# A decoder layer on one core: cross attention's projections as 16-bit products, and new places for every step

## Time and profile before

| | us |
|---|---|
| median of three runs | 619.71 |
| the profiled execution | 618.64 |
| its span | 616.8 |
| PE busy | 578.8 (94%) |
| DVE busy | 445.3 (72%) |
| ACT busy | 405.0 (66%) |
| POOL busy | 314.0 (51%) |

### The profile page before, as it was taken

How to read it: one execution, slowest core, us unless ns; L and a number is a source line. 1 busy time by engine, 2 the same in 40 slices (tenths; PEclk the granted TensorE clock), 3 DMA queues, 4 the chain that set the end, 5 groups by cost and what they waited for, 6 DMA issues and landing times. The chain is left out here.

```text
span 616.8 us, 17220 instructions
## 1 busy us (share of the span) xinstructions
PE 578.8 (94%) x6780; PEld 414.5 (67%) x6780; DVE 445.3 (72%) x1504; ACT 405.0 (66%) x520; POOL 314.0 (51%) x199
## 2 busy tenths in 40 slices
PE   6798888999999999999999999999999988899994
PEld 2544644777677877777677767786677756585664
DVE  2467476758897888888887889788878886267456
ACT  1425754796659765886579666976588657866661
POOL 5165432646357444665357544834566536155553
PEclk9898997999999999999999999999999999899999
DMA  6540111010200030002100120003000110000000
GB/s 179 157 138 27 46 49 43 5 30 1 72 14 10 2 91 28 22 2 62 56 21 3 46 73 19 4 2 108 10 22 3 35 55 4 2 19 2 2 18 18
DMA packets 31607, 23.08 MB, mean 37 GB/s; under 512 B 2808, under 2 KB 30216, under 8 KB 31528
## 3 DMA queue, kind: packets, MB, share of 16 engines
q1 hardware_dynamic: 23801, 16.59, 9.2%
q10 hardware_dynamic: 7375, 4.97, 2.7%
q0 software_dynamic: 352, 0.43, 0.4%
HBM read 13.90 MB, written 5.46 MB: 31 GB/s over the span
## 5 line engine op out<-in xcount | busy, mean ns | idle before, releaser
L540 POOL TENSOR_TENSOR gl<-g,gh 128x1024 f16<-128x1024 f32 x96 | 204.1, 2135 | 176.3 <-ACT gh L705 104.3
L716 ACT ACTIVATE g<-ps,b 128x512 f32<-128x512 f32 x256 | 168.5, 686 | 91.8 <-PE ps L1003 90.4
L1372 DVE SCALAR_TENSOR_TENSOR acc<-ps,cw,acc 128x128 f32<-128x128 f32 x448 | 125.9, 344 | 67.6 <-PE ps L1024 50.9
L1022 PE MATMUL ps<-w2h,gh 128*128 128x128 f16 x768 | 133.6, 219 | 1.9 <-DVE acc L1372 1.5
L1024 PE MATMUL ps<-w2h,gl 128*128 128x128 f16 x768 | 133.4, 219 | 0.0
L1023 PE MATMUL ps<-w2l,gh 128*128 128x128 f16 x768 | 133.4, 219 | 0.0
L1001 PE MATMUL ps<-x2h,w1h 128*128 128x512 f16 x256 | 98.6, 385 | 4.8 <-ACT g L716 4.8
L1003 PE MATMUL ps<-x2h,w1l 128*128 128x512 f16 x256 | 98.0, 383 | 0.0
L1002 PE MATMUL ps<-x2l,w1h 128*128 128x512 f16 x256 | 98.0, 383 | 0.0
L1022 PEld LDWEIGHTS ps<-w2h,gh 128*128 128x128 f16 x768 | 75.1, 98 | 18.1 <-issue 10.8
L1023 PEld LDWEIGHTS ps<-w2l,gh 128*128 128x128 f16 x768 | 75.1, 98 | 5.4 <-issue 1.6
(11 more groups left out here) (189 smaller groups left out, 900.2 us busy)
## 6 DMA issues: line engine op xcount, KB each, us to landing
q_rep<-q_parts SPq DMA_DIRECT2D x24, 128.0 KB
x<-in_x SPq DMA_DIRECT2D x8, 256.0 KB, 3.6
w_stage<-in_L_ffn_w ACTq DMA_DIRECT2D x1, 2048.0 KB, 10.9
q_swap<-q SPq DMA_DIRECT2D x16, 128.0 KB, 2.1
q_parts<-qx SPq DMA_DIRECT2D x16, 128.0 KB, 2.1
k_rep<-k_parts SPq DMA_DIRECT2D x24, 77.0 KB
out<-fin SPq DMA_DIRECT2D x7, 256.0 KB, 2.5
g<-in_L_ffn_w ACTq DMA_DIRECT2D x6, 256.0 KB, 3.1
```

Of the source, the lines that this page charges most:

```text
L540: pool.tensor_tensor(gl[:, j % SPLIT_RING, :, :], g32[:, e % RING, :, :], gh[:, j % SPLIT_RING, :, :], ALU.subtract).then_inc(s["lo"], 1)
L716: act.activation(g32[:, e % RING, h, :], bH[:, h, :], ACT.Gelu, bias=b1[:, e, h:h + 1], scale=1.0 / WS).then_inc(s["gelu"], 1)
L1022: pe.matmul(o, ghb, w2h[:, j, h, :], start=(h == 0), stop=False)
L1372: m = dve.scalar_tensor_tensor(out=(acc_all if e == E - 1 else acc)[:, b, :], in0=second_bank(f, e)[:, b * P:(b + 1) * P], scalar=cw[:, b, ...
```

## The change

The four projections no longer run in float32. The weights (`xw`) are split once into `xwh` (ACT, L643's place) and `xwl` (DVE), multiplied by WS = 256; ctx, x1 and the attention output are split as they leave PSUM: the high part by ACT in place of the copy, the low part by DVE in three new steps, `cx_l`, `x1_l` and `ao_l`. Each projection becomes three products into one sum: high by high, low weight by high, high by low. PE waits for the low parts where it waited for the copies. Since the sums carry the factor 256, what reads them divides: v in two DVE instructions instead of one (the operation takes one dimension less), the high parts of k and q in ACT's scale, their low parts in two DVE steps (first k or q in float32 into `k1` or `q1`, then the subtraction), y2 in its own instruction. `q1` lies in `y1`, so the norm waits for `qxl` of the group before. The exps stay whole.

All tables of places are new, and the counts of idle products with them. In the steady bodies the largest moves are: q's projection from place 63 to 55, its x1 transpose from 54 to 49, v from 46 to 53, k from 54 to 59; the query's steps of linear attention to 2 to 6; on PE the second transposed score from 35 to 34 and the third from 39 to 36, on ACT the exps from 32, 38, 39, 40 to 34, 36, 37, 40; ACT's conversion of x (`x_t`) from 3 to 0, ahead of the first gelu (place 1). In the first body ACT's first gelu (`q`) moves from place 15, behind the load places 6 and 8, to place 2, ahead of them; the loads of w2 move to 32, 35, 38 and 64. The diff, cut (of the tables the steady ones whole, of the others what is spoken of):

```diff
-PE_AT = dict(x_t=3, q=7, kv01=8, kv23=22, k_mean=28, kv=32, den=35, out=36, cx_t=43, v1=46, x1_t=54, k=54,
-             q_x=63, scores=(8, 8, 10, 12, 13, 14, 20, 20), max_t=26, scores_t=(29, 35, 39, 40), values=(39, 40,
-             42, 42), wo=55, x2_t=62, logits=0, c_t=57, b2=62, first=3, next=0, second=0, u_t=(43, 45), ao_t=49)
-ACT_AT = dict(x_t=3, q=5, kv23=25, cx_t=42, x1_t=54, k=55, q_x=63, max_t=27, scores_t=(32, 38, 39, 40), x2_t=62,
-              weights=0, c_t=61, gelu=1, high=3, u=(40, 45), ao_t=52)
-DVE_AT = dict(high=3, q=23, kv01=17, kv23=22, k_rot=26, k_mean=26, kv=31, den=33, out=33, norm1=37, norm2=41,
-              x1=49, v1=47, k=57, q_x=63, scores=(5, 8, 9, 11, 15, 16, 20, 20), max=22, pairs=(42, 47), wo=55,
-              x2=59, x2_t=61, logits=0, weights=3, cw=11, b2=61, combine=0, finish=51, q_sin=31, sums=31, xl=1,
-              cw_hl=42)
...
+PE_AT = dict(x_t=2, q=4, kv01=6, kv23=14, k_mean=24, kv=32, den=33, out=35, cx_t=42, v1=53, x1_t=49, k=59,
+             q_x=55, scores=(8, 9, 11, 15, 16, 20, 20, 23), max_t=28, scores_t=(32, 34, 36, 40), values=(36, 38,
+             41, 42), wo=50, x2_t=63, logits=0, c_t=59, b2=63, first=3, next=0, second=0, u_t=(42, 44), ao_t=47)
+ACT_AT = dict(x_t=0, q=2, kv23=24, cx_t=45, x1_t=51, k=58, q_x=55, max_t=30, scores_t=(34, 36, 37, 40), x2_t=63,
+              weights=0, c_t=60, gelu=1, high=3, u=(40, 44), ao_t=46)
+DVE_AT = dict(high=3, q=20, kv01=6, kv23=15, k_rot=25, k_mean=26, kv=29, den=30, out=34, norm1=34, norm2=38,
+              x1=43, v1=53, k=57, q_x=54, scores=(8, 10, 12, 14, 15, 17, 21, 22), max=23, pairs=(43, 43), wo=52,
+              x2=59, x2_t=63, logits=0, weights=2, cw=11, b2=61, combine=0, finish=41, q_sin=26, sums=29, xl=0,
+              cw_hl=30, cx_l=46, x1_l=51, ao_l=48)
...
-ACT_FIRST = dict(x_t=0, q=15, cx_t=24, kv23=22, k=32, x1_t=63, q_x=63)
...
-PE_FILL0 = dict(q=2, kv01=12, kv23=5, k_mean=1, kv=1, den=2, out=0, v1=6, k=0, x1_t=42, q_x=3)
-PE_FILL1 = dict(q=19, kv01=4, kv23=4, scores=0, max_t=0, scores_t=20, kv=2, den=0, out=0, k_mean=7, values=25,
-                wo=2, q_x=1, x2_t=6, v1=3, x1_t=1, u_t=31)
...
+ACT_FIRST = dict(x_t=0, q=2, cx_t=8, kv23=23, k=32, x1_t=59, q_x=63)
...
+PE_FILL0 = dict(q=9, kv01=6, kv23=3, k_mean=3, kv=0, den=0, out=0, v1=11, k=0, x1_t=47, q_x=6)
+PE_FILL1 = dict(q=22, kv01=1, kv23=4, scores=0, max_t=4, scores_t=9, kv=0, den=0, out=1, k_mean=0, values=24,
+                wo=3, q_x=8, x2_t=15, v1=4, x1_t=0, u_t=16)
...
-HIGH_W = (44, 56, 67, 68, 68, 76, 122)
-LOW_W = (76, 78, 80, 80, 92, 96, 124)
-SCALE_W = (119,)
-LOAD_W = (8, 29, 45, 57)
-W1_W = (6,)
-ROWS_W = (17, 59)
...
+HIGH_W = (40, 46, 72, 73, 73, 74, 86)
+LOW_W = (77, 78, 85, 88, 89, 102, 103)
+SCALE_W = (49,)
+LOAD_W = (32, 35, 38, 64)
+W1_W = (2,)
+ROWS_W = (9, 62)
...
                 if p == at["cx_t"]:
+                    if first_group(a):
+                        act.wait_ge(s["ld_xw"], 16 * 4)
+                        act.activation(xwh[:, :, :], xw[:, :, :], ACT.Copy, scale=WS).then_inc(s["i_xw"], 1)
                     since(act, "cx_tp", a + 1)
-                    act.copy(cx_t[:, :], bC[:, 0:B * CTX]).then_inc(s["cx_tc"], 1)
+                    act.copy(cxh[:, :], bC[:, 0:B * CTX]).then_inc(s["cxh"], 1)
                 if p == at["x1_t"]:
                     since(act, "x1_tp", a + 1)
-                    act.copy(x1_t[:, :], bC).then_inc(s["x1_tc"], 1)
+                    act.copy(x1h[:, :], bC).then_inc(s["x1h"], 1)
                 if p == at["k"]:
 
                     since(act, "k_p", a + 1)
                     since(act, "st_k", 16 * a)
-                    act.activation(kx[:, 0, :], bD[:, 0:B * CTX], ACT.Identity, bias=xbk[:, :]).then_inc(s["kxh"], 1)
+                    act.activation(kx[:, 0, :], bD[:, 0:B * CTX], ACT.Identity, bias=xbk[:, :], scale=1.0 / WS).then_inc(s["kxh"], 1)
                 if p == at["q_x"]:
                     since(act, "q_xp", a + 1)
                     since(act, "st_qh", 16 * a)
-                    act.activation(qx[:, 0, :], bC, ACT.Identity, bias=xbq[:, :]).then_inc(s["qxh"], 1)
+                    act.activation(qx[:, 0, :], bC, ACT.Identity, bias=xbq[:, :], scale=1.0 / WS).then_inc(s["qxh"], 1)
 
             def cross(g, p):
                 if p == at["max_t"]:
...
-                    act.copy(ao_t[:, :], bA).then_inc(s["ao_tc"], 1)
+                    act.copy(aoh[:, :], bA).then_inc(s["aoh"], 1)
...
-                    since(pe, "cx_tc", a + 1)
-                    pe.wait_ge(s["ld_xw"], 16 * 4)
-                    for b in range(B):
-                        m = pe.matmul(bD[0:CTX, b * P:(b + 1) * P], cx_t[:, b * CTX:(b + 1) * CTX], xw[:, 2, :], start=True, stop=True)
+                    since(pe, "cxl", a + 1)
+                    pe.wait_ge(s["i_xw"], 2)
+                    for b in range(B):
+                        o, tok = bD[0:CTX, b * P:(b + 1) * P], slice(b * CTX, (b + 1) * CTX)
+                        pe.matmul(o, cxh[:, tok], xwh[:, 2, :], start=True, stop=False)
+                        pe.matmul(o, cxh[:, tok], xwl[:, 2, :], start=False, stop=False)
+                        m = pe.matmul(o, cxl[:, tok], xwh[:, 2, :], start=False, stop=True)
                     m.then_inc(s["v1_p"], 1)
...
-                    pe.matmul(bD[:, 0:B * CTX], xw[:, 1, :], cx_t[:, :], start=True, stop=True).then_inc(s["k_p"], 1)
+                    pe.matmul(bD[:, 0:B * CTX], xwh[:, 1, :], cxh[:, :], start=True, stop=False)
+                    pe.matmul(bD[:, 0:B * CTX], xwl[:, 1, :], cxh[:, :], start=False, stop=False)
+                    pe.matmul(bD[:, 0:B * CTX], xwh[:, 1, :], cxl[:, :], start=False, stop=True).then_inc(s["k_p"], 1)
                 if p == at["q_x"]:
                     fill("q_x")
-                    since(pe, "x1_tc", a + 1)
-                    pe.matmul(bC, xw[:, 0, :], x1_t[:, :], start=True, stop=True).then_inc(s["q_xp"], 1)
+                    since(pe, "x1l", a + 1)
+                    pe.matmul(bC, xwh[:, 0, :], x1h[:, :], start=True, stop=False)
+                    pe.matmul(bC, xwl[:, 0, :], x1h[:, :], start=False, stop=False)
+                    pe.matmul(bC, xwh[:, 0, :], x1l[:, :], start=False, stop=True).then_inc(s["q_xp"], 1)
...
-                    since(pe, "ao_tc", g + 1)
-                    for b in range(B):
-                        m = pe.matmul(bB[:, b * P:(b + 1) * P], ao_t[:, b * P:(b + 1) * P], xw[:, 3, :], start=True, stop=True)
+                    since(pe, "aol", g + 1)
+                    for b in range(B):
+                        o, tok = bB[:, b * P:(b + 1) * P], slice(b * P, (b + 1) * P)
+                        pe.matmul(o, aoh[:, tok], xwh[:, 3, :], start=True, stop=False)
+                        pe.matmul(o, aoh[:, tok], xwl[:, 3, :], start=False, stop=False)
+                        m = pe.matmul(o, aol[:, tok], xwh[:, 3, :], start=False, stop=True)
...
+                    since(dve, "qxl", a)
...
-                    dve.tensor_tensor(of_heads(v_pad[:, :, :]), bD[0:CTX, :].rearrange("p (m j d) -> p m j d", j=2, d=HD),
-                                      bv[0:CTX, :, :].rearrange("p b (m j d) -> p (b m) j d", j=2, d=HD), ALU.add).then_inc(s["v1"], 1)
+                    for j in range(2):
+                        d = dve.scalar_tensor_tensor(out=of_heads(v_pad[:, :, :])[:, :, j, :], in0=bD[0:CTX, :].rearrange("p (m j d) -> p m j d", j=2, d=HD)[:, :, j, :],
+                                                     scalar=1.0 / WS, in1=bv[0:CTX, :, :].rearrange("p b (m j d) -> p (b m) j d", j=2, d=HD)[:, :, j, :],
+                                                     op0=ALU.mult, op1=ALU.add)
+                    d.then_inc(s["v1"], 1)
+                if p == at["cx_l"]:
+                    if first_group(a):
+                        dve.wait_ge(s["i_xw"], 1)
+                        dve.wait_ge(s["ld_b"], 16 * 3)
+                        dve.scalar_tensor_tensor(out=xwl[:, :, :], in0=xw[:, :, :], scalar=WS, in1=xwh[:, :, :], op0=ALU.mult, op1=ALU.subtract).then_inc(s["i_xw"], 1)
+                    since(dve, "cxh", a + 1)
+                    dve.tensor_tensor(cxl[:, :], bC[:, 0:B * CTX], cxh[:, :], ALU.subtract).then_inc(s["cxl"], 1)
+                if p == at["x1_l"]:
+                    since(dve, "x1h", a + 1)
+                    dve.tensor_tensor(x1l[:, :], bC, x1h[:, :], ALU.subtract).then_inc(s["x1l"], 1)
                 if p == at["k"]:
 
                     since(dve, "kxh", a + 1)
+                    dve.tensor_scalar(k1[:, :], bD[:, 0:B * CTX], 1.0 / WS, xbk[:, :], ALU.mult, ALU.add).then_inc(s["k1"], 1)
+                    since(dve, "k1", a + 1)
                     since(dve, "st_k", 16 * a)
-                    dve.scalar_tensor_tensor(out=kx[:, 1, :], in0=bD[:, 0:B * CTX], scalar=xbk[:, :], in1=kx[:, 0, :],
-                                             op0=ALU.add, op1=ALU.subtract).then_inc(s["kxl"], 1)
```

(23 more changed lines are left out.)

62 lines of the change are left out of this document (29 added, 33 removed).

## The result

The changed kernel takes 624.85 us in the median of 7 runs (618.94 to 626.34), the kernel before, on the same chip, 618.11 (613.89 to 620.84): a ratio of 1.0094, with a 95% interval of 1.0058 to 1.013. So it is slower by a little under 1%, about 6 us. The profiled execution took 621.17 us, span 619.2. The forecast was 623.5. It stood 3.8 above the 619.71 that was known for the kernel before; measured, the medians lie 6.7 apart (5.8 by the ratio) and the two profiled executions 2.4.

The account below looks back on a forecast made before the run. PE was taken to set the pace of the steady bodies. Start -3.4, first body +1.1, five steady bodies +7.0 and sixth -0.7 made +4.0 on 618.64, 622.6; forecast 623.5 for the median, range 611 to 629 us.

Parts of the forecast that it names:

- forecast case: Whole kernel: 621 to 627 us, chance 0.48, a third of it within 0.5% of the kernel before.
- Products: PE, each steady body: q, k, v and output projection as 16-bit products save 0.88 us.
- Rival D: Small products run no faster than the old passes, 111 ns and not 55.7: 630 us; chance 0.02.
- rival C: DVE becomes the bound, PE waiting at second products for its late combine: 629 to 635 us; chance 0.08.
- The waits: PE, steady body: start, expert 1, second and fourth transposed scores, ctx's transpose, expert 11; 3.4 us against 0.9, so +2.5.
- The rest of the walk: Steady body walked engine by engine in the new order: remaining difference besides products and waits, -0.2 us.
- The start: Before 158 us: first gelu at about 12 instead of 17.12, first x2 transpose 3.4 us earlier.
- Body 0: From the first x2 transpose to 157.97: waits of 3.0 us where about 2 were, +1.1 (0 to 2.5).
- The sixth body: The body without a next group: 64.89 to 64.2 us, same exps reordered, -0.7 (-3 to +2).
- A: Exps and x2's low part come in time, products and start save: 609 to 616 us; chance 0.23.
- B: Waits come but the start gains nothing, w1's later load holding up q's swap or weights: 626 to 629; chance 0.13.
- E: Passes cost PE the same and the order's waits cancel the start: 618 to 622 us; chance 0.06.

Follow-up runs that it names:

- tanh_behind_gelu: Changed kernel with ScalarE's tanh of the router moved behind expert 0's first gelu; 622.56 us, ratio 1.0072 to the kernel before.
- old_order_fitted: Changed kernel with the steady order of before, q's first VectorE step written to PSUM, low part of ao, tanh and logits re-placed; 618.37 us, ratio 1.0009.
- new_start_old_steady: Changed kernel with the steady tables of before, keeping the changed tables of the first bodies; 627.07 us, ratio 1.0166 to the kernel before.

## Why the prediction was right, and where two errors met

**Forecast.** 623.5 against 624.85, slower at 0.55, inside the forecast case. As a difference it was less good: +3.8 forecast, +6.7 between the medians measured, and the kernel before came 1.6 lower beside it than when I wrote. That the absolute number is off by 1.35 only is partly luck. The steady body, 67.8, was met (67.45 to 68.06), and in the profile it is what makes the kernel slower.

**Products.** -0.88 forecast, -0.89 measured, each term within 0.02. The pace of 55.7 ns holds for the small ones: eleven gaps from 279.17 to 279.78 are 55.5 each. Rival D falls. The 81 ns that *TensorE: Matmul & The Clock Gate* (the Trainium skill, section Back-to-back issue gap) gives for such a pair is not what these rows show.

**DVE.** +3.0 forecast, +3.2 measured. The step from PSUM with constant and bias took 0.75 for q and 0.53 for k, where I took 0.69 and, at the same rate, about 0.4. No second product waits for DVE in the new steady body but the one at its start; rival C did not come. That the all-SBUF step costs "the same" held only for its place.

**The waits.** Forecast 0.6, 0.87, 0.55, 0.52, 0.64 and 0.2, sum 3.4; measured 0.55, 0.86, 0.42, none, 0.41 and none, sum 2.24. The wait before expert 1 was read on two scales: from starts, as I read the 0.35 of before, it is 1.02 now, while the bracket of the trace has 0.19 before and 0.86 now. By either it grew by 0.67, where I had 0.52. Against before, then, waits grew by 1.5 and not 2.5. The first three are of the forecast's size and place, though the first is put down to the combine and not to x2's low part: b2's small product and the second products stand between them. The fourth transposed score does not wait at all, and ctx's transpose waits less, so the step that failed is the walk from exp 2 on. **The rest of the walk**, -0.2, was wrong by 0.8 the other way: scores, values and experts' products cost 0.62 more in the new order. That the scores stand one by one there and not in pairs is my guess at a reason, not shown. The two errors nearly cancel: that the body came out right is in part luck.

**The start.** First gelu at 12: it is at 11.54 (17.12 before). First x2 3.4 us earlier: in the profiled execution 0.1 (87.67 against 87.76), and 3.6 in tanh_behind_gelu, where the clock was nearly full. The head start is still there at the first transposed score, 59.33 against 64.70, and is nearly gone at the transpose of the attention output, 79.33 against 80.09; between them lie products at half clock and waits for exps. What the forecast left out is the granted clock of the first 90 us: the failed term is the -3.4.

**Body 0.** +1.1 forecast, -2.9 measured. The waits came (1.66 before expert 1, 1.26 for the row-maximum DMA). But the same body of the kernel before had waits too, 4.4 us in sum behind its first x2 (5.7 in the changed kernel) where I had counted about 2, one of them of 2.50 for q's DMA, and right behind that one PE ran at half clock, from about 96.5 to 103.3 us. The two rows are of before and of the changed kernel, from 88 us on:

```profile
88.00:155.00 67.00, 62.51 (x737) 43.83 (x735) 46.39 (x152) 47.05 (x60) 32.86 (x19) 0.95 0.09 26
```

```profile
88.00:155.00 67.00, 61.27 (x764) 44.76 (x763) 51.47 (x166) 49.66 (x63) 30.91 (x19) 1.00 0.09 26
```

The failed step was to count waits against "about 2" and no clock. Here too two errors met: -3.4 and +1.1 make -2.3, measured -3.0.

**The sixth body**: -0.7 forecast, -1.95 measured, inside its bounds.

**Rivals.** A had the saving and lost it to four waits, each real; old_order_fitted, with all but one covered, is the nearest thing to A and comes to the time of before, not below. B did not come in the profile: the second x2 stands before 158. For the median run, 3.7 us longer than the profiled one, it is not excluded that the gain of the start was gone. E fell with the slowdown.

## What to carry to other kernels

A written-out order is fitted to the durations of its steps: new products in the old order cost 2.2 to 2.6 us a body (1.0 of it my placing of one new step), and moving only the exps back 3 to 5. So price the order as a whole, step by step, and look at what each moved step had covered. On VectorE ask of each new instruction whether it reads only SBUF and what GpSimd is doing at that time; writing an intermediate to PSUM took a clash of 1.0 us away with no other change. Where a start is padded with idle products, treat its length as a range of some us, not as a number, and ask for the granted clock of the profiled execution beside that of the other runs before one start is compared with another.

## What the runs showed of the hardware

- A VectorE subtraction of 512 columns took 0.69 us alone and 1.72 or 1.73 beside a GpSimd instruction of 2.13 us in the steady bodies of new_start_old_steady, if both its inputs were in SBUF; with one input in PSUM 0.69 beside the same instruction. One of 308 columns took 0.48 alone and 1.29 beside it. Beside GpSimd's short rstd (128 by 4, 1.0 us) the all-SBUF form took 0.69 too.
- The same first bodies took 84.2 to 93.4 us, at mean granted clocks of 0.96 down to 0.81. The spans of seven runs of one kernel went from 617.1 us at a mean clock of 0.988 to 624.5 at 0.968.
- A product kept its 55.5 ns pace within a run of twelve, but q's third product took 0.37 us to the next start where second products followed it at once, and 0.22 in the changed kernel.
